# Two-layer sequence model on one core: state-space step sizes in two halves, and attention's value bias, late queries and first maxima on other engines

## The reference

```
1 attention, 16 heads of 8:  softmax(q k' / sqrt(8)) v Wo + bo    (value bias bv in v)
2 causal attention with rotated inputs, then a gate and the best 2 of 8 experts
3 state-space mixer (4 heads of 64, state 128) on rmsnorm(x):
    dt = softplus(u W_dt + dt_bias);  a = -exp(A_log) * dt;  dA = exp(a)
    h_t = dA_t h_{t-1} + dt_t B_t x_t ;  y_t = C_t h_t + D x_t
    x, B, C from a causal convolution over 4 tokens and silu; y times silu(z), rmsnorm, projection
  then a gated MLP of width 344
4 best 8 of 16 experts and a shared one
```

## Time and profile before

| | |
|---|---|
| median of three executions | 1815.76 us |
| the profiled execution | 1819.28 us |
| its span, first to last instruction | 1817.5 us |
| PE busy | 1681.8 us, 93% |
| DVE busy | 1268.1 us, 70% |
| ACT busy | 1193.8 us, 66% |
| POOL busy | 182.9 us, 10% |
| mean granted clock of TensorE | 0.962 |

### The profile page before, as it was taken

The page is one execution under the profiler, slowest core; times in us unless marked ns, Lnnn a source line. Parts: engine busy times, 40 slices in busy tenths (PEclk is TensorE's granted clock), DMA queues, the critical chain, the costliest instruction groups (busy, mean ns, idle before and its releaser), DMA issues. The chain is left out here.

```text
span 1817.5 us, 25943 instructions
## 1 busy us (share of the span) xinstructions
PE 1681.8 (93%) x10028; PEld 794.6 (44%) x10028; DVE 1268.1 (70%) x1804; ACT 1193.8 (66%) x2436; POOL 182.9 (10%) x171
## 2 busy tenths in 40 slices
PE   6999999999999999869999999999885798699997
PEld 3433333333333333245444444455553465344443
DVE  4888888888888888167788678574464366255555
ACT  4588888888888888845677777777546554333432
POOL 1000000000000000040000000111344000000100
PEclk9899999999999999989899999999988799699999
DMA  1000000000000000010000000000100000212220
GB/s 62 1 1 1 1 1 1 1 1 1 1 1 1 1 1 1 1 47 1 1 1 1 1 1 1 1 1 2 37 1 1 12 1 18 103 48 93 99 91 20
DMA packets 7274, 29.98 MB, mean 16 GB/s; under 512 B 680, under 2 KB 2736, under 8 KB 4848
## 3 DMA queue, kind: packets, MB, share of 16 engines
q1 hardware_dynamic: 7152, 28.33, 4.2%
HBM read 27.15 MB, written 1.18 MB: 16 GB/s over the span
## 5 line engine op out<-in xcount | busy, mean ns | idle before, releaser
L883 DVE TENSOR_REDUCE a_part_max<-a_ps 128x2 f32<-128x1024 f32 x512 | 602.5, 1221 | 86.9 <-PE a_ps L685 86.3
L868 ACT ACTIVATE a_probs<-a_ps 128x512 f32<-128x512 f32 x1024 | 533.1, 614 | 131.1 <-PE a_ps L781 128.6
L883 DVE TENSOR_REDUCE f_part_max<-f_ps 128x2 f32<-128x1024 f32 (+3 forms) x320 | 327.8, 1062 | 121.1 <-PE f_ps L685 65.2
L781 PE MATMUL a_ps<-a_q_shift,a_KA 64*128 64x512 f32 x1024 | 367.6, 448 | 3.6 <-POOL a_q_shift L664 2.4
L868 ACT ACTIVATE f_probs<-f_ps 128x512 f32<-128x512 f32 (+3 forms) x640 | 300.3, 539 | 99.8 <-PE f_ps L781 48.1
L781 PEld LDWEIGHTS a_ps<-a_q_shift,a_KA 64*128 64x128 f32 x1024 | 166.3, 187 | 290.8 <-ACT a_probs L868 275.1
L685 PE MATMUL a_ps<-a_KA,a_q_open 64*128 64x512 f32 x1024 | 278.0, 468 | 4.4 <-DVE a_part_max L883 3.8
L799 PE MATMUL a_psO<-a_probs,a_VA 128*32 128x512 f32 x2048 | 275.5, 610 | 3.9 <-ACT a_probs L868 3.9
L781 PE MATMUL f_ps<-f_q_shift,f_KA 64*128 64x512 f32 (+3 forms) x640 | 224.0, 435 | 4.7 <-POOL f_q_shift L664 2.2
L685 PE MATMUL f_ps<-f_KA,f_q_open 64*128 64x512 f32 (+3 forms) x640 | 170.4, 431 | 5.1 <-DVE f_part_max L883 4.3
L781 PEld LDWEIGHTS f_ps<-f_q_shift,f_KA 64*128 64x128 f32 x640 | 106.2, 188 | 150.1 <-ACT f_probs L868 138.4
(11 more groups left out here) (321 smaller groups left out, 1782.2 us busy)
## 6 DMA issues: line engine op xcount, KB each, us to landing
t_c_all<-c_rows SPq DMA_DIRECT2D x16, 1024.0 KB, 7.7
experts_w<-in_experts SPq DMA_DIRECT2D x1, 3264.0 KB, 10.5
W<-in_weights SPq DMA_DIRECT2D x1, 1574.0 KB, 6.2
out<-X SPq DMA_DIRECT2D x4, 256.0 KB, 6.8
K<-in_consts SPq DMA_DIRECT2D x1, 644.0 KB, 6.9
R<-in_rows SPq DMA_DIRECT2D x1, 530.0 KB, 5.9
W<-in_weights SPq DMA_DIRECT2D x1, 512.0 KB, 6.7
mx_conv_rows<-in_conv_rows SPq DMA_DIRECT2D x1, 512.0 KB, 3.5
```

The source lines that it names most:

```text
L781: mm = pe.matmul(bank(r)[:, lo:512], g.KA[rows, 2 * n + jp, P * s:P * s + P], q_shift[rows, u % 2, jp, lo:512], start=True, stop=not diag)
L868: nc.scalar.activation(probs[:, st % 2, j, lo:512], bank(r)[:, lo:512], ACT.Exp, scale=SCALE).then_inc(ring_read, 1)
L883: dve.tensor_reduce(part_max[:, 4 * q + 2 * jp:4 * q + 2 * jp + 2, c], ps1[:, k % 2, :, 0:b - a], AX_X, ALU.max).then_inc(max_read, 1)
```

## The change

In attention, the value bias is added by GpSimd on the copied values, no longer by a second product on TensorE. VectorE instead of GpSimd adds the first unit's maxima to its queries, and the first scores come one maximum behind the turn, not four. Of a late query block ScalarE writes one full copy and frees the bank with a no-op behind it; GpSimd writes the high part and subtracts; VectorE only cuts, eight maxima later.

A class `StepSizes` holds the step-size work for 8 of the 16 tiles. The first half of it is done in the norm stage: logits ahead of the last two transposes on TensorE, the chain on VectorE around the last normalisations, and ScalarE's exponentials and logarithm there. ScalarE's input of the mixer (`scale_u`) is now written ahead of the residual. The second half is done in the state-space loop: logits in chunk 1, the chain after chunks 1, 2 and 3, sums in chunk 5. The decays of chunk 0 move to the front.

```diff
-    EARLY, AHEAD = 2, 4
+    EARLY, AHEAD, FIRST_AHEAD, CUT_AFTER = 2, 4, 1, 8
...
+        if one[0] in ("shift", "cut"):
+            self.dve_work.append(one)
...
+                    late.append((self.CUT_AFTER, ("cut", self.units[u + 2][0])))
...
             late.append((self.EARLY, ("turn", u)))
+            if u == 0:
+                late.append((1, ("shift", 0)))
...
+        ahead = self.AHEAD if one[1] else self.FIRST_AHEAD
+        while n < ahead and at < len(stream):
...
-                for u in range(len(units)):
+                bias = g.r(bv).rearrange("p (h d) -> p h d", d=D).unsqueeze(1).to_broadcast([P, 4, H, D])
+                for b in range(NB):
+                    pool.wait_ge(ring_read, plan.query_at[("value", b)] + 1)
+                    pool.tensor_tensor(head_values(b), head_values(b), bias, ALU.add).then_inc(biased, 1)
+                def late_rest(i):
+                    k = plan.late_at[i]
+                    pool.wait_ge(late_full, k + 1)
+                    pool.tensor_copy(g.QP[:, 0, 512 * i:512 * i + 512], full[:]).then_inc(late_high, 1)
+                    pool.wait_ge(late_cut, k + 1)
+                    pool.tensor_tensor(g.QP[:, 1, 512 * i:512 * i + 512], full[:], cut[:].bitcast(F32),
+                                       ALU.subtract).then_inc(late_low, 1)
+                for u in range(1, len(units)):
+                    if u % NG == 2 and u + 2 < len(units):
+                        late_rest(units[u + 2][0])
                     pool.wait_ge(ring_read, plan.query_at[("turn", u)] + 1)
...
-                        pe.matmul(bank[:, P * x:P * x + P], tokens[:, P * t:P * t + P], g.w(wv), start=True, stop=False)
-                        mm = pe.matmul(bank[:, P * x:P * x + P], g.k("ident"), g.r(bv), start=False, stop=True)
+                        mm = pe.matmul(bank[:, P * x:P * x + P], tokens[:, P * t:P * t + P], g.w(wv), start=True, stop=True)
...
+                    if u == 0 and s % 4 == 0:
+                        pe.wait_ge(biased, s // 4 + 1)
...
-                        nc.scalar.activation(g.QP[:, 0, 512 * i:512 * i + 512], ps2[:, r % RING, :], ACT.Identity,
-                                             bias=g.c(bq)).then_inc(late_full, 1)
-                        nc.scalar.activation(full[:], ps2[:, r % RING, :], ACT.Identity, bias=g.c(bq)).then_inc(ring_read, 1)
+                        nc.scalar.activation(full[:], ps2[:, r % RING, :], ACT.Identity, bias=g.c(bq)).then_inc(late_full, 1)
+                        act.wait_ge(late_full, plan.late_at[i] + 1)
+                        act.nop().then_inc(ring_read, 1)
...
-                        dve.wait_ge(ring_read, plan.query_at[one] + 1)
+                        dve.wait_ge(late_high, k + 1)
                         dve.tensor_scalar(cut[:], g.QP[:, 0, 512 * i:512 * i + 512].bitcast(I32), HIGH_BITS, None,
                                           ALU.bitwise_and).then_inc(late_cut, 1)
-                        dve.wait_ge(late_cut, k + 1)
-                        dve.tensor_tensor(g.QP[:, 1, 512 * i:512 * i + 512], full[:], cut[:].bitcast(F32),
-                                          ALU.subtract).then_inc(late_low, 1)
+                        continue
+                    if one[0] == "shift":
+                        dve.wait_ge(ring_read, plan.query_at[("turn", 0)] + 1)
+                        for jp in range(2):
+                            dve.tensor_tensor(q_shift[:, 0, jp, :], q_open[:, 0, jp, :].bitcast(F32), shift_row[:, 0, :],
+                                              ALU.add).then_inc(q_shifted, 1)
...
+    def logits(self, pe, bank):
+        g = self.g
+        for t in range(8):
+            at = CONV - 1 + P * (self.first + t)
+            mm = pe.matmul(bank[:, MH * t:MH * t + MH], g.UT[:, at:at + P], g.w("mzdt")[:, DI:DI + MH], start=True, stop=True)
+        return mm
...
+    def raw(self, dve, src):
+        g, small, dt = self.g, self.small, self.g.dt[:, self.tok, :]
+        self.then(dve, dve.tensor_tensor(dt, src.rearrange("p (c h) -> p c h", h=MH), over_tiles(g.r("dtb"), 8), ALU.add))
+        self.then(dve, dve.tensor_scalar(small[:, 5], dt, -1.0, None, ALU.mult))
+        dve.tensor_tensor(small[:, 0], dt, small[:, 5], ALU.min).then_inc(self.raw_in, 1)
+    def exp_raw(self, act):
+        act.wait_ge(self.raw_in, 1)
+        act.activation(self.small[:, 0], self.small[:, 0], ACT.Exp).then_inc(self.raw_exp, 1)
+    def one_more(self, dve):
+        small, dt = self.small, self.g.dt[:, self.tok, :]
+        dve.wait_ge(self.raw_exp, 1)
+        self.then(dve, dve.tensor_scalar(small[:, 1], small[:, 0], 1.0, None, ALU.add))
+        dve.tensor_scalar(small[:, 3], small[:, 1], -1.0, None, ALU.add).then_inc(self.one_in, 1)
+        dve.wait_ge(self.one_in, 1)
+        self.then(dve, dve.tensor_scalar(small[:, 4], small[:, 3], 0.0, None, ALU.is_equal))
+        self.then(dve, dve.tensor_tensor(small[:, 3], small[:, 3], small[:, 4], ALU.add))
+        self.then(dve, dve.reciprocal(small[:, 5], small[:, 3]))
+        self.then(dve, dve.tensor_scalar(dt, dt, 0.0, None, ALU.max))
+    def log(self, act):
+        act.wait_ge(self.one_in, 1)
+        act.activation(self.small[:, 2], self.small[:, 1], ACT.Ln).then_inc(self.log_in, 1)
+    def step_size(self, dve):
+        g, small, dt = self.g, self.small, self.g.dt[:, self.tok, :]
+        dve.wait_ge(self.log_in, 1)
+        self.then(dve, dve.tensor_tensor(small[:, 2], small[:, 2], small[:, 5], ALU.mult))
+        self.then(dve, dve.tensor_tensor(small[:, 2], small[:, 2], small[:, 4], ALU.add))
+        self.then(dve, dve.tensor_tensor(small[:, 2], small[:, 2], small[:, 0], ALU.mult))
+        self.then(dve, dve.tensor_tensor(dt, dt, small[:, 2], ALU.add))
+        self.then(dve, dve.tensor_scalar(small[:, 3], dt, -1.0, None, ALU.mult))
+        dve.tensor_tensor(g.a[:, self.tok, :], small[:, 3], over_tiles(g.Aneg[:], 8), ALU.mult).then_inc(self.a_done, 1)
+    def decays(self, act, src, done):
+        dst = self.g.decay[:, :, self.tok, :].rearrange("p n c h -> p n (c h)")
+        act.activation(dst, src.rearrange("p (n k) -> p n k", n=3), ACT.Exp).then_inc(done, 1)
...
+                pe.wait_ge(ut_sb, 2)
+                sizes.logits(pe, ps[:, 3, :]).then_inc(dt_ps, 1)
                 turn_u(NB - 2)
+                sizes.sums(pe, ps[:, 3, 8 * MH:]).then_inc(sums_ps, 1)
                 turn_u(NB - 1)
...
+                def scale_u(b):
                     act.wait_ge(u_mean, b + 1)
...
+                nc.scalar.activation(g.Aneg[:], g.r("alog"), ACT.Exp).then_inc(aneg, 1)
+                sizes.exp_raw(nc.scalar)
                 apply2(NB - 1)
+                sizes.log(nc.scalar)
+                scale_u(NB - 2)
                 apply3(NB - 2)
                 copy_ut(NB - 2)
+                act.wait_ge(sums_ps, 1)
+                sizes.decays(nc.scalar, ps[:, 3, 8 * MH:32 * MH], decays)
+                scale_u(NB - 1)
                 apply3(NB - 1)
                 copy_ut(NB - 1)
...
+                dve.wait_ge(dt_ps, 1)
+                sizes.raw(dve, ps[:, 3, 0:8 * MH])
                 mean3(NB - 2)
                 mean2(NB - 1)
+                sizes.one_more(dve)
+                dve.wait_ge(aneg, 1)
+                sizes.step_size(dve)
                 stats3(NB - 1)
                 mean3(NB - 1)
...
+                    if c == 1:
+                        sizes.logits(pe, s_bank(c)[:, P + DI:])
+                    if c == 5:
+                        sizes.sums(pe, s_bank(c)[:, P + DI + 8 * MH:])
...
-                for t in range(NT):
-                    mm = pe.matmul(ps[:, 6, MH * t:MH * t + MH], g.UT[:, U0 + P * t:U0 + P * t + P],
-                                   g.w("mzdt")[:, DI:DI + MH], start=True, stop=True)
-                mm.then_inc(dt_ps, 1)
                 project(0, COPY_B)
                 project(0, COPY_C)
+                decays_of(0)
                 convolve(0, 0)
                 convolve(0, 1)
-                pe.wait_ge(a_done, 1)
-                for n, name in enumerate(("upto", "after", "ones")):
-                    mm = pe.matmul(ps[:, 7, C * MH * n:C * MH * (n + 1)], g.k(name),
-                                   a[:].rearrange("p c h -> p (c h)"), start=True, stop=True)
-                mm.then_inc(sums_ps, 1)
                 turn_x(0, 0)
                 gate(0, 0)
                 turn_x(0, 1)
                 gate(0, 1)
                 turn_b(0)
-                for c in range(4):
+                for c in range(1, 4):
                     decays_of(c)
                 scores(0)
...
+                spread_a(0)
                 act.wait_ge(pad_clear, 1)
                 copy_pad(0, 0)
                 copy_pad(0, 1)
-                nc.scalar.activation(Aneg[:], g.r("alog"), ACT.Exp).then_inc(aneg, 1)
-                act.wait_ge(raw_in, 1)
-                nc.scalar.activation(small[:, 0], small[:, 0], ACT.Exp).then_inc(raw_exp, 1)
```

(29 more changed lines are left out.)

## The result

The changed kernel took 1805.69 us (median of 5 runs, 1801.66 to 1806.22) beside 1814.79 us for the kernel before (5 runs, 1814.04 to 1816.18): ratio 0.9942, 95% interval 0.9929 to 0.9955. It is faster: by 9.1 us as the difference of the medians, by 10.5 us as the ratio has it. Forecast were 1801.7 us and a range of 1793 to 1809. The two profiled executions took 1819.28 and 1806.22 us, 13.1 apart.

The account below looks back on a forecast made before the run. TensorE, busy 93% of the span, was taken as the bound, VectorE at attention's starts. Terms -7.1, 0, -2.4, +1.9, -12.5 and +6.05 summed to -14.1 us, applied to the median 1815.76: 1801.7 us, range 1793 to 1809.

Parts of the forecast that it names:

- value bias: Both attention stages: dropping TensorE's second value product gains 7.1 us, GpSimd's additions being hidden; bounds 6 to 7.6.
- first maxima: Start of attention: VectorE's shift additions and earlier first scores cancel, 0 us; bounds 5 us gained and 3 lost.
- late queries: Six attention units with late query work: less ScalarE and VectorE work gains 0.4 us each, 2.4 in all; bounds 0 and 4.
- end of the norm stage: Last blocks of the norm stage: six small operations held up by GpSimd, and reordering, cost 1.9 us; bounds 0.3 and 3.
- state-space start: Before the state-space loop: logits, spreads and waits removed, convolutions 6.6 us in, not 10.1; 12.5 us gained.
- first two passes of the loop: State-space loop: second-half logits, a later turn_x(1,0), step sizes and second-pass sums cost 6.05 us.
- 1 (the dips vanish): Attention's starts: earlier scores keep TensorE's clock up, 5 us more gained, 1796.7 us; chance 14%.
- 2 (the loop pays double): Loop: TensorE's clock falls while waiting for turn_x(1,0), five us of delay become eleven, 1807.7 us; chance 12%.
- 3 (start and loop cancel): State-space half doesn't gain, and the norm stage adds 1.9: -7.6 us, 1808.2 us; chance 8%.
- 4 (half clock holds itself): Attention's first unit: TensorE stays at 1.2 GHz, about +10 us if all of unit 0 in both stages, 1826; chance 3%.
- 5 (all cancels): Whole change: bias or step sizes are waited for where they were free; time within 0.2% of before; chance 3%.

Follow-up runs that it names:

- taps kernel: The combined kernel with GpSimd's taps product at the state-space start split into two halves of 128 columns; 1797.03 us, ratio 0.9877 to the kernel before.
- The halves: The changed kernel with only VectorE's two shift additions kept (scores behind four maxima), 1803.56 us; with only the early scores kept (additions on GpSimd), 1804.10 us.
- loop kernel: The changed kernel with the second half of the step sizes begun ahead of the state-space loop; 1801.94 us, ratio 0.9896 to the kernel before.
- combined kernel: The loop kernel with first maxima undone and the norm stage's last six small operations behind block 3's statistics; run twice, 1800.76 and 1800.38 us.

## Why the prediction came out as it did

| step | predicted | in the traces |
|---|---|---|
| value bias | -7.1 | -6.3 |
| first maxima | 0 (-5 to 3) | +2.7 |
| late queries | -2.4 | -2.2 |
| end of the norm stage | +1.9 | +1.3 |
| state-space start | -12.5 | -13.0 |
| first two passes of the loop | +6.05 | +4.9 |
| sum | -14.1 | -12.6 |

The right column comes from the table, the joins left out: the value bias from A and C of the kernels with the first maxima undone (96.37 and 95.25) against the three with the old attention (means 99.44 and 98.51); the others as told above, the start as F of before (40.78) less that of changed (27.77), norm stage and loop as E, G and H. The two profiled executions differ by 13.1.

**Value bias**: right in mechanism (the maxima beside the value blocks follow each other in 1.51 us, TensorE bounds them, and the reductions still take 1.23), and 6.3 lies within the bounds of 6 to 7.6. No run has this edit alone; the size is a difference of means, and with the taps kernel's A and C it would be 6.9.

**First maxima**: the step that failed, and the largest miss, 2.7 us in A and C. The prediction saw that VectorE is the bound there and that the reductions fall behind by 1.7 us, and then set off one maximum fewer against one score product more as "nothing won, nothing lost". But where VectorE bounds, a maximum fewer is a reduction that is still to be done, and a score product that TensorE did earlier, in time in which it would have waited anyway, is worth next to nothing. The halves show both: additions +2.6, early scores +0.1. Charged to the bounding engine in full, two additions in each of two stages are 2.6 us (4 of 0.65). That this is the very number measured is partly luck: A and C repeat only to a us, and VectorE's wait for the row (0.3 us a stage) would come on top. What the miss cost the whole kernel isn't shown, as told above.

**Late queries**: right, 0.3 to 0.4 us for each of six units. GpSimd's copy took 0.62 us instead of the 1.25 assumed, with no consequence.

**Norm stage**: right in mechanism (a VectorE operation held up by GpSimd's addition, the statistics queued behind), 0.6 less in size. The logarithm came in the first quarter of the second addition and its user was stretched to 1.06 us rather than kept out until the end; the output normalisation, put at 0.5, cost what is left, 0.3.

**State-space start**: right. The convolutions started 5.9 us in instead of 6.6 (6.4 or 6.5 in eight other traces). That TensorE there waits for the taps (0.49 us in this trace) was seen; that this wait has a clock of its own to lose was not.

**Loop**: right in mechanism, 1.15 less in size. turn_x(1,0) came 16.9 us in instead of 17.7, as VectorE reached one_more after 14.1 us and not 15.3. Second pass +0.62 (0.75 predicted).

**From the sum to the time.** The sum was 1.5 us off, the time 4.0. The rest is the step that carried the sum over to the median: it took the profiled execution's 3.5 us above the median for an offset that both kernels share. The changed kernel's profiled execution lay 0.5 above its own median. In the second set, where the kernel before had its median at 1819.73, the difference of the medians was 12.4 us, near the table's sum; as the joins vary by more than the two differ, that they agree so well is luck in part. Why the kernel before ran at 1814 to 1816 in the first set and near 1819 in the others isn't settled.

**The rivals.** 1 (the dips vanish): no, they last ten us in both stages as before. 2 (the loop pays double): no, the granted clock stays at 1.00 from 1430 to 1462 us. 3 (start and loop cancel): no, 13.0 against 4.9. 4 (half clock holds itself): no, it ended after ten us. 5 (all cancels): no. In the loop kernel's trace the table load was followed at once by the activation again (1436.55 plus 1.28, activation at 1437.85): no drain like the 1.38 us that the Trainium skill names (ScalarE: Activation LUTs, What ACT_TABLE_LOAD costs).

## What to carry to other kernels

Find the engine that bounds a stretch, and charge work that moves onto it in full, whatever it frees elsewhere; earlier work for an engine that would wait anyway counted for nothing here. Compare traces stretch by stretch, but add up the stretches between them as well: what one stretch wins can be gone at the next join. When an operation waits on another engine's chain, look for what that chain is queued behind before blaming the operation: here the logarithm and its two loads were free once its input came early. And a wait of TensorE just behind a rise of its clock is worth a look: in two traces it cost itself and then 1.7 us at the half clock.

## What the runs showed of the hardware

- VectorE and GpSimd hold each other up beyond what I had assumed: the three multiply-adds of the first convolution on VectorE took 4.49 us beside GpSimd's taps product (4.29 to 4.30 in eight other traces), where the second three took 2.33. GpSimd's product took 2.35 us beside nothing of VectorE's in the kernel before, and 2.44 to 2.83 in those eight. The small two-input operation took 1.06 us for 0.19.
- The clock fell to half right after it had risen, behind one wait of 2.16 us: 1.7 us lost on 16 products, in both traces of the combined kernel; in eight traces in which the decays ahead had still run at the half clock (1.56 to 1.91 us instead of 1.02) and the wait was 0.4 to 1.3 us, the same products took 7.11 us.
- So the norm stage's better order won 1.0 us, and the stretch behind it gave 1.7 back. Which of the two differences (earlier clock, longer wait) decides isn't shown: the kernel without the wait was traced once, with the late clock. And a long wait isn't all there is to it: the second trace of the combined kernel and that of the taps kernel fell to half once more 20 to 23 us into the stage, behind waits of at most 0.8 us, where the first trace of the combined kernel and the loop kernel's, with the same waits, did not.
